# Mixture of experts: each routed expert computes only its own tokens

## The reference

```
shared = (silu(x @ sw1.T) * (x @ sw3.T)) @ sw2.T
s = sigmoid(x @ router_w.T + t_emb @ router_t_w.T);   idx = top_k(s + router_bias, 2)
gates = s[idx] / (sum(s[idx]) + eps)
H_e = gelu(x @ rw1[e].T)              # 256 -> 128, 8 experts
routed = sum over the two chosen e of gates_e * (H_e @ rw2[e].T)
out = (shared + routed) / 3
```

## Time and profile before

| | us |
|---|---|
| median of 3 runs | 1235.5 (1235.4 to 1236.3) |
| the profiled execution's own time | 1231.9 |
| its span in the trace | 1229.8 |
| second mixture, first router matmul to the last maximum | 804.8 to 1114.4 |

### The profile page before, as it was taken

How to read it: one execution, slowest core, us unless ns; L and a number is a source line. 1 busy time by engine, 2 the same in 40 slices (tenths; PEclk the granted TensorE clock), 3 DMA queues, 4 the chain that set the end, 5 groups by cost and what they waited for, 6 DMA issues and landing times.

```text
span 1229.8 us, 31887 instructions
## 1 busy us (share of the span) xinstructions
PE 1102.4 (90%) x10420; PEld 847.4 (69%) x10421; DVE 898.7 (73%) x3007; ACT 550.1 (45%) x1743; POOL 246.3 (20%) x285
## 2 busy tenths in 40 slices
PE   6777777877878999999999999789999999996898
PEld 5665665665657888888888888646776567763355
DVE  5676676776776688965555555468898988988887
ACT  4555555555554333333333333362445424444276
POOL 1002112112115675243333333300000000001000
PEclk9999999999999999999999999989999999998999
DMA  7222332332334577444444444241000000000024
GB/s 179 78 71 86 100 94 85 100 98 81 99 96 113 94 168 141 88 73 61 63 62 63 64 64 64 50 124 69 2 1 1 0 1 1 1 1 1 1 34 105
DMA packets 98711, 82.31 MB, mean 67 GB/s; under 512 B 58529, under 2 KB 88354, under 8 KB 98594
## 3 DMA queue, kind: packets, MB, share of 16 engines
q1 hardware_dynamic: 82946, 57.98, 18.6%
q0 software_dynamic: 15648, 22.86, 10.7%
HBM read 41.18 MB, written 33.60 MB: 61 GB/s over the span
## 4 chain that ended last, share of the span: by engine, by line
PE 77%; DVE 10%; ACT 8%; issue 3%; DMA 1%; SPq 0%; POOL 0%; DVEq 0%
PE ps L572 24%; PE ps L1129 17%; PE ps L1139 17%; PE ps L1686 7%; DVE ps L1615 6%; PE ps L1691 4%; ACT work L1539 4%; ACT ps L1534 3%; DVE imax L1008 2%; PE ps L1656 2%; PE ps L917 1%; PE ps L922 1%; PE ps L888 1%; PE ps L1664 1%; DVE W L836 1%
## 5 line engine op out<-in xcount | busy, mean ns | idle before, releaser
L1157 ACT ACTIVATE lane<-ps,b_now 128x256 f32<-128x256 f32 x312 | 147.7, 474 | 260.0 <-PE ps L1129 246.0
L1129 PE MATMUL ps<-lane,W 128*128 128x256 f16 x1872 | 212.8, 274 | 0.9 <-issue 0.8
L1139 PE MATMUL ps<-W,lane 128*128 x1872 | 210.9, 273 | 0.2
L1129 PEld LDWEIGHTS ps<-lane,W 128*128 x1872 | 183.7, 98 | 23.8 <-issue 1.7
L1139 PEld LDWEIGHTS ps<-W,lane 128*128 128x128 f16 x1872 | 182.6, 98 | 22.3 <-issue 0.8
L1686 PE MATMUL ps<-work 128*128 128x16 f16 x2048 | 98.9, 177 | 86.1 <-ACT work L1539 85.5
L1686 PEld LDWEIGHTS ps<-work 128*128 128x128 f16 x2048 | 76.2, 107 | 137.8 <-ACT work L1539 136.4
L572 PE MATMUL ps<-W,work 128*128 128x512 f16 x768 | 168.5, 381 | 0.1
L1298 POOL DMA_INDIRECT results<-lane,dest x78 | 124.7, 1598 | 217.0 <-DVE lane L1212 184.3
L1224 DVE TENSOR_TENSOR lane<-lane 128x256 f16<-128x256 f32 x312 | 133.3, 427 | 10.8
L572 PEld LDWEIGHTS ps<-W,work 128*128 128x128 f16 x768 | 74.8, 98 | 90.1 <-issue 1.9
(11 more groups left out here) (213 smaller groups left out, 1466.7 us busy)
## 6 DMA issues: line engine op xcount, KB each, us to landing
stage<-in_w1T SPq DMA_DIRECT2D x16, 512.0 KB, 3.6
stage<-in_w2T SPq DMA_DIRECT2D x16, 512.0 KB, 4.1
b_now<-in_b SPq DMA_DIRECT2D x39, 128.0 KB
work<-in_zT SPq DMA_DIRECT2D x32, 128.0 KB, 2.1
results<-in_xn SPq DMA_DIRECT2D x32, 128.0 KB
W<-results SPq DMA_DIRECT2D x8, 512.0 KB, 3.8
rows<-work SPq DMA_DIRECT2D x8, 257.0 KB, 5.2
out<-W SPq DMA_DIRECT2D x4, 512.0 KB, 4.0
```

The lines of the kernel that those rows point to most:

```text
L1129: last = pe.matmul(ps[:, f % 4, 0:ST], of_e(W1[:, bass.ds(e, 1), a, k, f * P:(f + 1) * P]), xT[:, p, b, k], start=(i == 0 and k == 0), sto ...
L1139: last = pe.matmul(ps[:, 4 + q, 0:D], hid[:, a, f, q * P:(q + 1) * P], of_e(W2[:, bass.ds(e, 1), b, f]), start=(i == 0 and f == 0), stop=( ...
L1157: act.activation(v4[:, f % 4], ps[:, f % 4, 0:ST], ACT.Relu, bias=b1_now[:, p, f:f + 1], scale=A_SCALE / W_SCALE).then_inc(l1_v, 1)
```

## The change

The first stages and the network at the end stay as they are. The second mixture is laid out in three phases.

Routing phase: four steps of two groups. `mix_route_op` has 32 DVE operations per step for 1024 tokens (tiles of 128 x 64 or 128 x 128 where the old ones were 128 x 32), with the gates, a rank per token (`mix_ranks` on PE) and the row's slot in the new buffer `mrows`. POOL then scatters each token's row of 1040 bytes (both halves and 4 numbers: token, first choice, gates) to the regions of its two experts: 8 indirect DMAs per group, 64 in all. ACT reuses one of four row buffers only after its scatters landed (`moved`). PE interleaves 8 of the shared branch's units per step, and 12 after the last step, with three PSUM banks in turn. After the last step SP copies 256 empty rows behind each region's end.

Tile phase: 39 tiles of 256 rows. SP loads a tile's rows (266 KB) and its expert's two weights (256 KB, from a copy in DRAM). PE transposes the rows, computes the first layer (6 matmuls of 256 columns) and the second (6 of 256), with three quarters of a shared unit per tile in between. DVE reads the gates and the destinations (`tile_gates`) and multiplies (`tile_out`); POOL scatters the 256 results with two indirect DMAs to a row per token and choice in `mresults`. Rows, weights, outputs and destinations have three buffers.

Tail: SP loads `mresults` (1 MB per group, three buffers), and DVE adds both rows of a token to the shared output and takes the maxima (`combine`), beside the last 22 shared units.

```diff
+XBUFS = 4
+PAIR = 2 * GT
+STEPS_M = GROUPS // 2
+TILE_BUFS = 3
+MIX_OPS = 32
+UNITS = 2 * HSC + GT
+STEP_UNITS = 8
+BRIDGE_UNITS = 12
+TILE_UNITS = 30
+LATE = 6
+COMBINE = (0, 1, 2, 6, 3, 4, 5, 7)
...
+            for m in range(STEPS_M):
+                v = STEP_UNITS * m
+                for g in (2 * m, 2 * m + 1):
+                    router(g)
+                for k in range(3):
+                    shared(v + k)
+                mix_ranks(m)
+                for k in range(3, 6):
+                    shared(v + k)
+                for g in (2 * m + 2, 2 * m + 3):
+                    if g < GROUPS:
+                        transposes(g)
+                    shared(v + 4 + g - 2 * m)
+            for v in range(STEPS_M * STEP_UNITS, FIRST_TILE_UNIT):
+                shared(v)
...
+            def tile_transposes(n):
+                pe.wait_ge(mrow_in[n % TILE_BUFS], 16 * (n // TILE_BUFS) + 16)
+                if n:
+                    pe.wait_ge(mT, n)
...
+            def tile_first(n):
+                pe.wait_ge(mT, n + 1)
+                pe.wait_ge(mw_ready[n % TILE_BUFS], 16 * (n // TILE_BUFS) + 16)
+                if n >= 2:
+                    pe.wait_ge(mgelu, n - 1)
...
+            def tile_second(n):
+                pe.wait_ge(mlo, n + 1)
+                if n >= 2:
...
+                last.then_inc(m2_ps, 1)
...
+            tile_transposes(0)
+            for n in range(SLOT_TILES):
+                if n < SLOT_TILES - 1:
+                    tile_transposes(n + 1)
+                tile_first(n)
+                for v in tile_units(n):
+                    shared(v)
+                if n:
+                    tile_second(n - 1)
+            tile_second(SLOT_TILES - 1)
+            for v in range(TAIL_UNIT, UNITS * GROUPS):
+                shared(v)
...
+                if g >= XBUFS:
+                    act.wait_ge(moved[b], 2 * GT * 16 * (g // XBUFS))
+                act.activation(xsn[:, b, :, 0:D], x1[:, GT * g:GT * g + GT], ACT.Copy, scale=A_SCALE).then_inc(xn_hi, 1)
...
+            tile_T(0)
+            for n in range(SLOT_TILES):
+                if n < SLOT_TILES - 1:
+                    tile_T(n + 1)
+                act.wait_ge(m1_ps, n + 1)
+                if n >= 2:
+                    act.wait_ge(mlo, n - 1)
+                act.activation(mv[:, n % 2], ps[:, 1 + n % 2, 0:ST], ACT.Gelu, scale=1.0 / MIX_SCALE).then_inc(mgelu, 1)
+                act.wait_ge(mgelu, n + 1)
+                if n >= 2:
+                    act.wait_ge(m2_ps, n - 1)
+                act.activation(mhid[:, n % 2, 0], mv[:, n % 2], ACT.Copy, scale=V_SCALE).then_inc(mhi, 1)
...
+            for m in range(STEPS_M):
+                v = STEP_UNITS * m
+                mix_route_op(dve, m, 0)
+                shared(v)
+                for n in range(1, 9):
+                    mix_route_op(dve, m, n)
+                shared(v + 1)
+                for n in range(9, 15):
+                    mix_route_op(dve, m, n)
+                shared(v + 2)
+                for n in range(15, 28):
+                    mix_route_op(dve, m, n)
+                shared(v + 3)
+                for n in range(28, MIX_OPS):
+                    mix_route_op(dve, m, n)
+                for g in (2 * m + 2, 2 * m + 3):
+                    shared(v + 2 + g - 2 * m)
+                    if g < GROUPS:
+                        input_lo(g)
+                for k in (6, 7):
+                    shared(v + k)
+            mix_table(dve)
+            for v in range(STEPS_M * STEP_UNITS, FIRST_TILE_UNIT):
+                shared(v)
...
+            def tile_gates(n):
+                b = n % TILE_BUFS
+                tail = lambda k: mrow[:, b, :, D + k:D + k + 1]
+                mine = mtile_f[:, 0, n]
+                dve.wait_ge(mrow_in[b], 16 * (n // TILE_BUFS) + 16)
+                if n >= TILE_BUFS:
+                    dve.wait_ge(mstored[b], SQ * 16 * (n // TILE_BUFS))
+                dve.scalar_tensor_tensor(mdest[:, b], tail(1), mine, tail(0), ALU.is_equal, ALU.add).then_inc(mdest_set, 1)
+                dve.scalar_tensor_tensor(mmask[:, b], tail(1), mine, tail(3), ALU.is_equal, ALU.mult).then_inc(mgate_step, 1)
+                dve.wait_ge(mgate_step, 2 * n + 1)
+                dve.tensor_tensor(mgate[:, b], mmask[:, b], tail(2), ALU.add).then_inc(mgate_step, 1)
+
+            def tile_lo(n):
...
+            def tile_out(n):
+                b = n % TILE_BUFS
+                dve.wait_ge(m2_ps, n + 1)
+                dve.wait_ge(mgate_step, 2 * n + 2)
+                dve.tensor_tensor(mout[:, b], ps[:, 3 + n % 2].rearrange("p (q d) -> p q d", q=SQ),
+                                  mgate[:, b].broadcast_to([P, SQ, D]), ALU.mult).then_inc(mout_set, 1)
+
+            dve.wait_ge(mtable, 3)
+            tile_gates(0)
+            for n in range(SLOT_TILES):
+                tile_lo(n)
+                for v in tile_units(n):
+                    shared(v)
+                if n < SLOT_TILES - 1:
+                    tile_gates(n + 1)
+                if n:
+                    tile_out(n - 1)
+            tile_out(SLOT_TILES - 1)
+
+            def combine(at):
+                g, b = COMBINE[at], at % TILE_BUFS
+                yg = y[:, GT * g:GT * g + GT]
+                if g < LATE:
+                    dve.wait_ge(routed_in[b], 16 * (at // TILE_BUFS) + 16)
+                    link(dve, dve.tensor_tensor(yg, yg, routed[b][:, :, 0], ALU.add))
+                else:
+                    dve.wait_ge(unit_read, output_unit(g, GT - 1) + 1)
+                link(dve, dve.tensor_tensor(yg, yg, routed[b][:, :, 1], ALU.add))
+                dve.tensor_reduce(ymax[:, g:g + 1], yg.rearrange("p q d -> p (q d)"), AX.X, ALU.max).then_inc(combined, 1)
+
...
+            for v in range(TAIL_UNIT, first_late):
+                shared(v)
+            for at in range(3):
+                combine(at)
+            for v in range(first_late, first_late + GT):
+                shared(v)
+            combine(3)
+            for n in range(3):
+                for v in range(first_late + GT + 2 * n, first_late + GT + 2 * n + 2):
+                    shared(v)
+                combine(4 + n)
+            for v in range(last_late, UNITS * GROUPS):
...
+        def mixture_pool(pool):
+            rows_flat = mrows_d.rearrange("r s n -> (r s) n")
+            for g in range(GROUPS):
+                pool.wait_ge(router_step, MIX_OPS * (g // 2 + 1))
+                pool.wait_ge(xn_lo, g + 1)
+                pool.wait_ge(tok_set, g + 1)
+                for k in range(2):
+                    for q in range(GT):
+                        at = GT * (g % XBUFS) + q
+                        pool.indirect_dma_start(out=rows_flat, in_=xrow[:, g % XBUFS, q], in_offset=None,
+                                                out_offset=bass.IndirectOffsetOnAxis(ap=mslot_of[:, k, at:at + 1], axis=0))\
+                            .then_inc(moved[g % XBUFS], 16)
+            for n in range(SLOT_TILES):
+                b = n % TILE_BUFS
+                pool.wait_ge(mout_set, n + 1)
+                pool.wait_ge(mdest_set, n + 1)
+                for q in range(SQ):
+                    pool.indirect_dma_start(out=mresults_d, in_=mout[:, b, q], in_offset=None,
+                                            out_offset=bass.IndirectOffsetOnAxis(ap=mdest[:, b, q], axis=0))\
+                        .then_inc(mstored[b], 16)
+
...
+            for e in range(E):
+                end = sp.value_load(mends[0:1, e:e + 1], min_val=0, max_val=ROOMS * ST - ST)
+                sp.dma_start(rows_flat[bass.ds(end, ST)], pads_d[e]).then_inc(padded, 16)
...
+            def load_tile(n):
+                b = n % TILE_BUFS
+                r = sp.value_load(mroom_of[0:1, n:n + 1], min_val=0, max_val=ROOMS - 1)
+                e = sp.value_load(mexpert_of[0:1, n:n + 1], min_val=0, max_val=E - 1)
+                if n >= TILE_BUFS:
+                    sp.wait_ge(mT_ps, n - TILE_BUFS + 1)
+                    sp.wait_ge(mgate_step, 2 * (n - TILE_BUFS) + 2)
+                    sp.wait_ge(mdest_set, n - TILE_BUFS + 1)
+                sp.dma_start(mrow[:, b], mrows_d[bass.ds(r, 1)].rearrange("a (q p) n -> p (a q) n", p=P))\
+                  .then_inc(mrow_in[b], 16)
+                if n >= TILE_BUFS:
+                    sp.wait_ge(m2_ps, n - TILE_BUFS + 1)
+                sp.dma_start(mw_words[:, b], rweights_d[bass.ds(e, 1)].rearrange("a p n -> p (a n)")).then_inc(mw_ready[b], 16)
...
+            for i in range(XBUFS):
+                sp.wait_ge(moved[i], 2 * GT * 16 * ((GROUPS - 1 - i) // XBUFS + 1))
+            for n in range(SLOT_TILES):
+                load_tile(n)
+            for i in range(TILE_BUFS):
+                sp.wait_ge(mstored[i], SQ * 16 * ((SLOT_TILES - 1 - i) // TILE_BUFS + 1))
+            for at in range(GROUPS):
+                g, b = COMBINE[at], at % TILE_BUFS
+                if at >= TILE_BUFS:
```

(53 more changed lines are left out.)

658 lines of the change are left out of this document (369 added, 289 removed).

## The result

The changed kernel took **1368.8 us** (median of four runs, 1362.8 to 1371.3) beside 1235.9 (1235.4 to 1236.7) for the kernel before on the same chip: a ratio of 1.107 (1.103 to 1.1105). It is slower, as forecast, but the time lies 49 us above the forecast and 7 above the range. The profiled execution took 1362.8 us.

A forecast was written before the change was run, and what follows sets the result against it. PE was taken to bound the kernel before, and uncovered store waits the tiles after. From 804.8 us, 4.2 + 106.5 + 5.2 + 219.6 + 16.7 + 42.0 gave 394.2 against 309.6, so 1235.5 + 84.6 = 1320 us; range 1282 to 1362.

The forecast's parts named there:

- first routing operation: Start of the second mixture's routing phase: 809 us, 4 us later because ACT prepares two groups before the routers.
- last scatter issued: End of POOL's 64 routing scatters, following each other at 1.27 us within steps of 22: issued at 908.8 us.
- tile pitch T: Tile phase: each iteration contains a whole store, 2.8 us plus L, so 6.1 us, 36 times.
- the routing phase's sum: Routing phase of four steps of 22 us with POOL's scatters: 106.5 us in all.
- steps start at 809, 831, 853, 875: Routing phase: four steps, slots ready 13.5 us after each begins, the rest of a step 8.5 us.
- DVE's step and POOL's queue run at nearly one pace, and each covers the other: Routing phase: 16 scatters take 20.3 us against a step of 22; removing either alone would win 2 us per step.
- The way to the first store: Between routing and tiles: scatters landed at 912, rows at 915.5, then 5.2 us to the first `tile_out` at 920.7.
- The tile phase: Tiles: `tile_gates` waits for an earlier tile's store, nothing covers it; 36 iterations, 219.6 us.
- L: Tile loop: time from issue to landing of a tile's second result scatter, taken at 3.3 us.
- The tail: After the tiles: reading results back, additions, maxima and last outputs, with waits 42 us, last maximum at 1199.
- PE's own sum: PE's work in the second mixture: 207 us where it was 304; 97 us won if PE stayed the bound.
- Rival 4: Routing phase: scatters at 1.59 us each, 64 costing 20 us more; only widens the range, no chance of its own.

The follow-up runs named there:

- e13: The changed kernel without any edit, as a control on a chip of the first kind (kernel before about 1233 us): 1323.3 us.
- e14: Changed kernel with the 64 scatters writing only 16 bytes per row to a small table, tiles using fixed rows and destinations; first kind of chip: 1315.1 us.
- e15: Changed kernel with a POOL memset of 16 columns (0.125 us) before each of the 64 scatters; first kind of chip: 1327.8 us.
- e17: Changed kernel with six destination and gate buffers, empty-row copies in 16 pieces, rows loaded ahead of weights, 16-column memsets before scatters; first kind: 1226.9 us, ratio 0.9952.
- e9: The changed kernel without any edit, on a chip of the second kind (kernel before 1235.9 to 1239.8 us): 1369.9 us, ratio 1.1055.
- e11: Changed kernel with a POOL memset of 128 x 512 before each of the 64 scatters; second kind of chip: 1350.9 us.
- e12: Changed kernel with six instead of three buffers for destinations and gates, the store wait moved to `tile_out`; second kind of chip: 1313.0 us, ratio 1.0596.

## Why the prediction came out as it did

The changed kernel's last maximum ended at 1245.6, 131.2 us after the old one (1114.4), where 84.6 were forecast. Term by term, with e13 (1323.3 us, first kind) beside it:

| term (us) | forecast | measured | e13 |
|---|---|---|---|
| first routing operation | 809 | 812.7 | 807.4 |
| last scatter issued | 908.8 | 946.7 | 908.4 |
| from it to the first store | 12.9 | 25.2 | 18.0 |
| first store to last store | 226.9 | 220.6 | 226.6 |
| tile pitch T | 6.1 | 5.92 | 6.10 |
| last store to the last maximum's end | 50.4 | 53.2 | 53.1 |

- **The failing step is the routing phase's sum**, "steps start at 809, 831, 853, 875", and in it that "DVE's step and POOL's queue run at nearly one pace, and each covers the other". It took the two queues as independent. On the chips of the second kind POOL's queue delays the signals that DVE, PE and ACT wait for: DVE starts a step late, POOL then has nothing to scatter, and the cover is gone on both sides (POOL's idle time before L1327 is 83.7 us). From the first routing operation to the last scatter it is 133.9 us, where 99.8 were forecast and e13 has 101.0: 34 us of the miss of 47.
- **Before the stage** the trace of the result is late as well: the last store of the first mixture is issued at 797.7, where the trace of before has 792.9 and e13 792.5, and the first routing operation comes 3.7 us later than forecast. 1.7 us of it are there when the scan ends and 2.5 more come in the first mixture's first tile, where POOL issues eight scatters back to back and PE stops twice (1.59 and 0.67 us). e13 has neither stop. Since the trace of before is of the first kind, this compares two kinds of chip, and is not shown to be a cost of the change: the kernel before also takes 3 to 7 us more on the second kind.
- **The way to the first store** was undersized by 5 us even without late signals. The rows were there on time (first transposes at 915.1 in e13, forecast 915.5), but PE waits 1.2 us more for the second tile's rows, ACT loads a table before the first gelu (1.28 us), and PE transposes three tiles ahead of the first `tile_out`, not two; eight transposes take 1.03 us there and 0.61 later. The granted clock is 0.50 from 915 to 920 us, the lower of its two levels, and 0.95 from 920 to 926. With late signals it is 12 too short: PE still had 36 matmuls of shared units to do from 950.84 to 961.45.
- **The tile phase was right** in mechanism and size. L was taken at 3.3; DVE went on 3.2 us after the second issue in the mean, and with the 2.7 us of the rest (0.96, 1.27 and 0.47) that is the 5.92. In e13, which has the landing times, the scatters landed in 2.8 us at the median. The Trainium skill's estimate for this landing (DMA: Bandwidth & Descriptors, Anatomy of one DMA; about 2.3 us for 128 KB) is half a microsecond short of e13's median and 0.1 of its least, 2.4: that trace agrees only for the quickest landings.
- **The tail** was 3 us dearer than forecast, on both kinds, and the forecast had 1.3 us too many before it: it let L begin after the sixth of the last scatters, though L starts with the issue.
- **PE's own sum** was low: 207 us forecast, and PE is busy for 268 of the 436 us from 810 on, at a granted clock of 0.82 where the earlier trace rows have 0.99. The 97 us that the change was to take from PE were 37. It set no time here, since PE waits in every window.
- **The sum** thus holds, within 6 us and with errors of both signs in its terms, where the signals are not late: 1323.3 in e13 against 1320, or 90.1 us more than the kernel before on the same chip against 84.6. The range left out what the result's chip did, since it gave the coupling between POOL's queue and other engines' waits no term at all. Rival 4 had the right place (scatters in the routing phase) and the wrong quantity: most scatters kept their 0.97 us and 0.30 gap (mean 1.01). Its price was also too low: 1.59 us and a gap of 0.30 are 1.89 for each, which over 64 ends 35 us later than the forecast's 908.8, not 20. That this is near the measured 38 is chance.

**Still open.** Whether the bytes or the instructions of the scatters delay the signals, whether a gap of 0.13 us is enough, and why chips differ: the runs that could tell (e14, e15, e17) fell on chips without the effect. A rival that no run tests is the recording of the trace itself. Every execution here was recorded, and where signals are late records are missing: of the 1,024 landings of the 64 scatters the trace's semaphore records hold 1,019 in e13, but 254 in the result and 274 in e9, and 861 in e11, where the memsets stand between. The late starts and the longer times are real in these executions; whether they would be there without the recording is not known. Instructions that came late are not the cause: no instruction fetch was outstanding in the stretches of waiting of 834.6 to 845, 864.5 to 875.6 and 898 to 915 us. (The Trainium skill, Runtime: NRT & Kernel Launch, Instruction fetch mechanics, calls such fetches mostly hidden; the trace agrees.)

## What to carry to other kernels

A wait on a store must not stand ahead of the operation that feeds the next store on the same engine: moving it one call later, with six buffers for what it guards, took 57 us out of 39 tiles (e12 against e9). When tiles come from DRAM, order the loads by when they are wanted (rows for the transposes ahead of weights), or the next limit is a load. Two queues that "cover each other" are a sum without reserve; ask what one of them does to the other's signals. Compare traces of before and after from the same chip, and time the kernel on more than one before deciding.

## What the hardware showed unexpectedly

Runs of 16 back-to-back indirect DMAs on POOL (0.97 us each, 0.30 apart) hold up semaphore updates of PE and of DMAs, and PE's own issue, until gaps between them: 4 to 10 us late per step in the result, 45 us of DVE's waiting in e9. This is what recorded executions show; whether the recording has a part in it is open. On chips of the other kind, with the same program and the same 1.27 us from scatter to scatter, signals arrive within 0.1 us. The kernel before, whose second mixture has no scatters, differs between the kinds by 3 to 7 us, the changed one by 45 to 48. A memset of 0.54 us and its wait between scatters (pitch 1.8) removes the delay and makes both kinds equal, at about 30 us more than the unedited kernel on the first kind.
